# An attention block and a mixture of experts on one core: the passage to the experts' phase rearranged

## What is computed

```python
# attention over the 16 heads of one token, 16 channels each
q = (layernorm(x) @ Wq.T).reshape(B, N, 16, 16)
k = (ctx @ Wk.T).reshape(B, N, 16, 16);  v = (ctx @ Wv.T).reshape(B, N, 16, 16)
attn = softmax(einsum('bnhd,bngd->bnhg', q, k) * SCALE)
h = x + einsum('bnhg,bngd->bnhd', attn, v).transpose(0, 2, 1, 3).reshape(B, N, C) @ Wp.T + bp
# shared expert of width 512, and 16 experts of width 128, two per token
t = layernorm(h)
shared = (silu(t @ sfc1.T) * (t @ sfc2.T)) @ sfc3.T
top_w, top_idx = top_k(t @ gate_w.T, 2);  top_w = softmax(top_w)
moe = sum over the two chosen e of  top_w * (silu(t @ w1[e].T) @ w2[e].T)
out = h + moe + shared
```

## Time and profile before

| | us |
|---|---|
| median of 3 runs (1761.17 to 1768.10) | 1765.73 |
| the profiled execution | 1761.86 |
| its span, first to last instruction | 1760.0 |
| TensorE busy | 1481.3 (84%) |
| VectorE busy | 1337.1 (76%) |
| GpSimd busy | 1318.4 (75%) |
| ScalarE busy | 720.3 (41%) |
| the last chunk's rows ready, plan begins | 1245 |
| first load of the experts' rows | 1272.1 |
| first load of the sums | 1299.9 |
| first scatter of the experts' phase | 1305.9 |

### The profile page before, as it was taken

How to read it: one execution, slowest core, us unless ns; L and a number is a source line. 1 busy time by engine, 2 the same in 40 slices (tenths; PEclk the granted TensorE clock), 3 DMA queues, 4 the chain that set the end, 5 groups by cost and what they waited for, 6 DMA issues and landing times.

```text
span 1760.0 us, 50739 instructions
## 1 busy us (share of the span) xinstructions
PE 1481.3 (84%) x17109; PEld 1302.0 (74%) x17110; DVE 1337.1 (76%) x3378; ACT 720.3 (41%) x1346; POOL 1318.4 (75%) x1253
## 2 busy tenths in 40 slices
PE   5499999999999999999999999998667777677774
PEld 4487787887788777788877888876557777677774
DVE  7577887888888888888888878888536666566663
ACT  3244444544445444444444444443223333233331
POOL 5277777777777777777778778776668888788886
PEclk9699999999999999999999999999879999899997
DMA  8788888889987898888888887886578888688783
GB/s 199 131 200 194 180 170 175 179 194 198 174 181 162 191 213 175 175 173 176 200 196 175 169 174 175 201 170 144 203 261 255 254 252 254 183 260 252 245 257 114
DMA packets 945836, 344.76 MB, mean 196 GB/s; under 512 B 824089, under 2 KB 898731, under 8 KB 940289
## 3 DMA queue, kind: packets, MB, share of 16 engines
q1 hardware_dynamic: 901680, 216.53, 60.1%
q0 software_dynamic: 33600, 92.91, 14.8%
q10 hardware_dynamic: 10512, 34.79, 6.1%
HBM read 200.37 MB, written 148.15 MB: 198 GB/s over the span
## 4 chain that ended last, share of the span: by engine, by line
PE 40%; DVE 19%; POOL 14%; issue 14%; ACT 5%; SPq 4%; DMA 3%; POOLq 1%; DVEq 1%; ACTq 0%
PE bank_a L1178 4%; PE bank_a L1193 4%; POOL sums L535 4%; POOL out L535 4%; POOL xn_lo L527 4%; PE bank_y L1178 4%; ACT xn L645 3%; DVE w_sb L800 3%; PE bank_a L1180 3%; PE bank_a L1179 3%; PE bank_y L1180 3%; PE bank_y L1179 3%; DVE ctx_lo L912 3%; DVE v_area L1132 2%; PE bank_u L1178 2%
## 5 line engine op out<-in xcount | busy, mean ns | idle before, releaser
L414 POOL DMA_INDIRECT slots<-xn,slot_i x256 | 281.7, 1101 | 97.9 <-issue 54.8
L1132 DVE SCALAR_TENSOR_TENSOR v_area<-bank_y,tail,v_area 128x256 f32<-128x256 f32 x288 | 120.6, 478 | 151.1 <-PE bank_y L1180 125.7
L1178 PE MATMUL bank_y<-w_hi,xn_hi 128*128 x288 | 97.9, 340 | 119.7 <-POOL xn_lo L527 108.4
L535 POOL DMA_INDIRECT sums<-v_area,tail x144 | 145.2, 1008 | 46.3 <-issue 34.5
L535 POOL DMA_INDIRECT out<-v_area,tail x144 | 145.1, 1008 | 42.3 <-issue 34.9
L722 ACT ACTIVATE th<-bank_z 128x512 f32<-128x512 f32 x72 | 43.1, 598 | 289.6 <-PE bank_z L1441 282.5
L1178 PEld LDWEIGHTS bank_y<-w_hi,xn_hi 128*128 128x128 f32 x288 | 57.4, 199 | 134.6 <-issue 134.6
L423 POOL DMA_INDIRECT sums<-v_area,slot_i x128 | 128.1, 1001 | 33.0 <-issue 29.9
L1178 PE MATMUL bank_a<-w_hi,ctx_hi 128*128 128x256 f32 (+1 forms) x320 | 107.8, 337 | 43.8 <-DVE ctx_lo L912 43.7
L1178 PE MATMUL bank_y<-wsh_out_hi,hid_hi 128*128 128x256 f32 x512 | 143.1, 280 | 1.3 <-POOL hid_lo L445 1.3
L1179 PE MATMUL bank_y<-wsh_out_lo,hid_hi 128*128 128x256 f32 x512 | 142.8, 279 | 0.0
(11 more groups left out here) (223 smaller groups left out, 5254.2 us busy)
## 6 DMA issues: line engine op xcount, KB each, us to landing
k_area<-slots SPq DMA_DIRECT2D x288, 129.0 KB
v_area<-sums SPq DMA_DIRECT2D x288, 128.0 KB
kv_dram<-w_sb SPq DMA_DIRECT2D x32, 1024.0 KB, 4.3
x_sb<-in_x_in SPq DMA_DIRECT2D x32, 512.0 KB
ctx_sb<-in_ctx_t SPq DMA_DIRECT2D x32, 512.0 KB
q_dram<-q_sb SPq DMA_DIRECT2D x32, 512.0 KB, 5.8
k_area<-kv_dram SPq DMA_DIRECT2D x256, 64.0 KB
w_sb<-q_dram SPq DMA_DIRECT2D x256, 64.0 KB
```

The costliest lines, as they stand in the source:

```text
L414: pool.indirect_dma_start(slots[j], bass.IndirectOffsetOnAxis(ap=slot_i[:, par, j, i:i + 1], axis=0), row_of[j][:, i, :], None).then_inc(S ...
L535: pool.indirect_dma_start(target, bass.IndirectOffsetOnAxis(ap=tail[:, r, t, 1 - j:2 - j].bitcast(u32), axis=0), y_ring[:, r, t, :], None, ...
L1132: st = nc.vector.scalar_tensor_tensor(out=y_ring[:, r, t, :], in0=Y[t // 2][:, t % 2 * C:(t % 2 + 1) * C], scalar=tail[:, r, t, j:j + 1], ...
L1178: mm(out, lhs_hi, rhs_hi, start=start, stop=False)
```

## The change

It touches the passage alone.
- **The padding's plan first.** VectorE works out `pad_at_i` right after the last chunk's routing, ahead of `shared_act(0, 1)`. The rest of the plan runs after these two, up to the scans (L1065), then comes `shared_act(2)`, then the rest.
- **Only to the tile's end.** Five more small instructions (`pad_in_tile`, `pad_past`) find which blocks of 8 lie past the end of the expert's last tile, and add FAR to their index, so that they are left out.
- **Pass by pass.** `pads` takes one array at a time. Rows of FIRST are padded first, its sums after the last `hid_split`; rows of SECOND after the base scatters, its sums after the two `inner_split` of quad 0. SyncE's `load_x` waits for `rows_padded1` alone, `load_sums` for `based` and `sums_padded1`, and `padded0` is waited for before the second pass.
- **w2's split** is one VectorE instruction, between `copy_w1(0)` and `base_sum`.
- **Places.** `pad_flat` moves to `v_flat` from 5120, `base` to `k_flat` from 7168, `slot_row` from 7168 to 6656.

```diff
-        slot_row = k_flat[0:1, 7168:7168 + TOP * QUADS * 4].bitcast(i32)
+        slot_row = k_flat[0:1, 6656:6656 + TOP * QUADS * 4].bitcast(i32)
...
-        base = v_flat[:, 5120:5120 + BPC * C].rearrange("p (i f) -> p i f", i=BPC)
+        base = k_flat[:, 7168:7168 + BPC * C].rearrange("p (i f) -> p i f", i=BPC)
...
-        pad_flat = v_flat[:, 0:PAD * ROW]
+        pad_flat = v_flat[:, 5120:5120 + PAD * ROW]
...
             sp.wait_ge(S["no_tile_stored"], 2 * 16 * TOP)
-            sp.wait_ge(S["padded1"], 2 * 16 * 3)
+            sp.wait_ge(S["rows_padded1"], 16 * 3)
             sp.wait_ge(S["scattered1"], 16 * BPC * CHUNKS)
...
             sp.wait_ge(S["based"], 16 * BPC * CHUNKS)
-            sp.wait_ge(S["padded0"], 2 * 16 * 3)
+            sp.wait_ge(S["sums_padded1"], 16 * 3)
...
             sp.wait_ge(S["scattered0"], 16 * BPC * CHUNKS)
+            sp.wait_ge(S["padded0"], 2 * 16 * 3)
...
-            pads(1)
+            pads(slots[FIRST], ROW, FIRST, "rows_padded1")
             hid_split(CHUNKS - 1, range(1, SB))
+            pads(sums[FIRST], C, FIRST, "sums_padded1")
             scatter(CHUNKS - 1, 1, SCATTERS[BPC:])
             scatter_base(CHUNKS - 1, 1, range(BPC))
-            pool.wait_ge(S["w2_hi_ready"], 1)
-            pool.wait_ge(S["u_full"], SB * CHUNKS)
-            half = slice(0, E * C // 2)
-            nc.gpsimd.tensor_tensor(w2_lo[:, half], w2_sb[:, half], w2_hi[:, half], ALU.subtract).then_inc(S["w2_split"], 1)
-            pads(0)
+            pads(slots[SECOND], ROW, SECOND, "padded0")
...
             for part in range(2):
                 inner_split(0, 0, part)
+            pads(sums[SECOND], C, SECOND, "padded0")
...
             weigh(c)
-            shared_act(c, range(2), False)
...
+            done(nc.vector.tensor_single_scalar(pad_block[:, :], pad_block[:, :], P // PAD - 1, ALU.bitwise_and))
+            done(nc.vector.tensor_copy(pad_in_tile[:, :], pad_block[:, :]))
+            for g in range(2):
+                st = nc.vector.tensor_scalar(pad_past[:, g, :], pad_in_tile[:, :], pad_row[:, 5:6], float(P // PAD - 1 - g * PAD), ALU.add, ALU.is_ge)
+            done(st)
...
+            done(nc.vector.scalar_tensor_tensor(out=places[:, :, 1:3], in0=pad_past[:, :, :].rearrange("p g j -> p j g"), scalar=float(FAR),
+                                                in1=places[:, :, 1:3], op0=ALU.mult, op1=ALU.add))
             nc.vector.tensor_copy(pad_at_i[:, :], pad_at[:, :]).then_inc(S["pad_at_ready"], 1)
-            shared_act(c, range(2, 3), False)
+            shared_act(c, range(2), False)
...
                 done(nc.vector.tensor_tensor_scan(last_tile[:, j, :], tiles_f[:, j, :], tiles_n[:, j, :], 0.0, ALU.mult, ALU.add))
+            shared_act(c, range(2, 3), False)
...
             copy_w1(0, 0, True)
-            base_sum(CHUNKS - 1, 1, False)
             dve.wait_ge(S["w2_hi_ready"], 1)
             dve.wait_ge(S["u_full"], SB * CHUNKS)
-            half = slice(E * C // 2, E * C)
-            nc.vector.tensor_tensor(w2_lo[:, half], w2_sb[:, half], w2_hi[:, half], ALU.subtract).then_inc(S["w2_split_2"], 1)
+            nc.vector.tensor_tensor(w2_lo[:, :], w2_sb[:, :], w2_hi[:, :], ALU.subtract).then_inc(S["w2_split"], 1)
+            base_sum(CHUNKS - 1, 1, False)
```

24 lines of the change are left out of this document (12 added, 12 removed).

## The result

| | before | changed |
|---|---|---|
| median of five runs, us | 1765.26 | 1753.71 |
| lowest and highest | 1761.17 to 1768.10 | 1749.59 to 1757.22 |
| the profiled execution | 1761.86 | 1757.22 |
| its span | 1760.0 | 1755.4 |

The changed kernel takes 0.9936 of the time before, with a 95% interval of 0.9913 to 0.9958: 11.5 us less. On another chip the same two kernels gave 1752.36 against 1763.18, a ratio of 0.993 (0.9912 to 0.9948). The forecast was 1749.2 within 1744 to 1757: the time lies in the range, and the gain is 11.5 us where 16.5 were forecast. The gain is clear of noise, but small: 0.4 to 0.9%.

What follows compares the result with a forecast made beforehand. GpSimd's queue was taken to bound the loop, whose first scatter would move from 1305.9 to 1289.4. The profiled 1761.86 less 16.5 gives 1745.4, plus 3.9 to the median: 1749.2 us, range 1744 to 1757.

Steps and rivals of the forecast that it cites:

- The mechanism and the sign: GpSimd's queue is the loop; its first scatter starts 16.5 us earlier, and this is carried to the program's end.
- The padding's plan: VectorE's padding plan, moved ahead of two activations: 2.98 us plus 0.8 for new operations, from 1245.6 to 1249.4.
- The rest of the plan: VectorE's remaining plan after the activations: 8.9 us shrink to 5.9, ready at 1258.1, 2.6 us earlier.
- The held-up scatter: GpSimd's first scatter of the second list, held up by VectorE's split of w2, ends at 1270.3 instead of 1266.7.
- the rival without it: VectorE's split of w2 leaves GpSimd alone; loop starts at about 1286, gain 20, 1745.7 us; chance 0.13.
- From the loads of the sums to the first scatter: At the loop's start, first load of the sums to first scatter takes 6.0 us, as in the kernel before.
- the rival of the transfers: Padding of the second list beside the sums' loads makes them 2 to 6 us late: 1751 to 1755 us; chance 0.18.
- The start-up: Rival: quads 0 to 2 each cost 3 us over 6.1, competing with base work; gain 7.5, 1758 us; chance 0.10.
- The signs of being wrong: Prediction wrong if the loop's first scatter comes after 1296 or a pass takes over 222 us.
- The sum: Whole program: 1761.86 less 16.5 gives 1745.4; with 3.9 to the median, 1749.2 us, 0.9% faster.
- The likeliest case: Whole program: gain 14.5 to 18.5 us, time 1747 to 1751; chance 0.55.
- the slower case: Rival: loop settles at a longer period; at 0.36 us a quad the kernel is 0.5% slower, 1775 us; chance 0.04.

Runs made afterwards that it cites:

- the repeat: The changed kernel once more, unaltered, on another chip: 1752.36 us, ratio to the kernel before 0.9930.
- e2: Changed kernel with the padding of FIRST's sums issued ahead of the last three splits of `hid`: 1750.27 us, ratio to the kernel before 0.9936.
- e5: Kernel before with only the w2 part: one VectorE split, GpSimd's half gone: 1758.60 us, ratio to the kernel before 0.9960.
- e1: Changed kernel with VectorE's split of w2 in eight instructions instead of one: 1751.74 us, ratio to the kernel before 0.9939.
- e3: Changed kernel with all padding of SECOND moved behind quad 3 of the first pass: 1752.08 us, ratio to the kernel before 0.9945.
- e9: Changed kernel with w2's split in eight, FIRST's sums padded early, and quad 4's rows loaded behind quad 1's sums: 1748.46 us, ratio to the kernel before 0.9916.
- e11: Changed kernel with plan, block and w2 parts undone, leaving the padding's order and waits; on a slower chip: ratio to the kernel before 1.0009.
- e12: Changed kernel with only the padding's order and waits left, run again, on a slower chip: ratio to the kernel before 1.0005.

## Why the prediction was right, and where it was wrong

**The mechanism and the sign: right in the main.** The loop's start moved forward, and the second pass kept its length. That an earlier start is carried to the end of the program did not hold: of 12.2 us, and 15.0 in the repeat, 7.6 and 7.9 arrived. The waits fell in the order that was forecast: the first load of x now leaves 2.4 us after the tables (28.5 against 26.0), the loads of the sums after the base scatters alone.

**The padding's plan: right**, 10.0 us against 10.5.

**The rest of the plan: the term was mis-sized.** The step said that 8.9 us shrink to 5.9 and the plan is ready 2.6 us earlier; it was 0.35. The step moved VectorE's work and assumed that each operation keeps its duration. But in the new order VectorE reaches line 1077 while GpSimd splits `hid`, and 0.16 us became 2.73 (e2 shows both sides of it); line 1063 lost 1.1 us more. The padding's plan shows the same in small: its 2.98 us held 12 operations, not 14, and 0.5 us of hold-up at line 1041, so the new one came out at 10.0 instead of 10.5. The forecast counted the hold-up in one direction, a DMA issue behind VectorE's split, and not in the other. The 2.3 us went through to tables, x loads and w2's split; at the end of the base scatters 1.5 us of them were left.

**The held-up scatter: right**, 4.22 us, ending 0.84 us after VectorE's 1269.75 + 4.41, where 0.8 had been read from the earlier trace rows; so the rival without it falls. It stands in other traces too: 4.41 us for one issue in e5, again ending 0.84 us after the split, and 1.5 us for each of three issues in e1. The other direction shows in the 2.73 us of line 1077 beside GpSimd's splits. What part of an issue has to wait, none of them shows.

**From the loads of the sums to the first scatter: the step that failed.** I carried over 6.0 us from a stretch in which nothing else was transferred; it took 10.4, and 8.3 in the repeat. This is the rival of the transfers, which had 0.18 and would have given 1751 to 1755. Its cause is the one it named, the padding of SECOND (e3: 6.5), and its size, 4.4 and 2.3 us, lay in the 2 to 6 us that it gave. The forecast moved the padding past the loads and priced only GpSimd's side of that.

**The start-up: a second loss that I had left at 0.10.** It cost 4.5 us in the first pass and 7.1 in the repeat, 9 in the rival, which left a gain of 7.5. The rival gave another cause, quads 0 to 2 slowed one by one. What the runs show is a wait: the first ring is loaded by one queue in a fixed order, and the fifth quad's rows (quad 4) stand behind 16 loads that now take 14.24 us. e9 moves them, and the loss goes down to 1.7. Both losses seem to have one root, the padding of SECOND beside these 16 loads: without it they took 8.89 us, and TensorE began quad 4's transposes at 58.0 us after T instead of 65.2 (e3).

**The signs of being wrong.** The prediction was to be wrong if a pass took over 222 us, and the first took 222.7, and 225.3 in the repeat: by its own sign the passes of equal length are refuted. The other sign, a first scatter after 1296, came at 1296.72 by the clock of the trace, but 3 us of that are the later end of the chunks; from T the limit is 57.05, and it came at 54.8.

**The sum.** From T the forecast was 16.5 us: 4.35 were lost at the loop's start, and 4.5 in the first pass; 7.6 were left in the trace, and 11.5 (7.4 to 15.4) in the timed runs. In the repeat it was 1.5 and 7.1, with 7.9 left, and 10.8 us in the timed medians. Each time some 3 us of the timed gain stand in no mark of the passage. They lie within the interval and the wandering of the chunks, but what they are is not shown. The likeliest case as I gave it, 1747 to 1751, did not hold; the range did, since two rivals came true in part. That the time lies in it is in part luck: the 7.6 to 7.9 us of the marks, taken from 1765.73, would give 1758, outside. (A slip in the slower case: 25.3 / 72 is 0.35 us a quad, not 0.36.)

**The parts.** Undoing one part at a time cost 0.9 us (plan), 0.3 (blocks) and nothing (w2) at the end, and w2 alone on the kernel before brought 3.2. They overlap: each takes work off the end of the same queue, and once one thing else is last, the others bring nothing. That would leave most of the gain to the order and the waits of the padding, but only if the other three don't replace one another. The runs that were to show it, e11 and e12, don't settle the end, and their loop started only 6.6 us earlier instead of 12.2 to 15.0. So how the gain divides among the parts stays open.
